# The order of maxima, scores and values on TensorE in two attention layers, and which wait an exponential carries

## What is computed

```python
scores = jnp.einsum('bhqd,bhkd->bhqk', q, k) / jnp.sqrt(jnp.float32(HEAD_DIM))
causal = jnp.tril(jnp.ones((t, t), dtype=bool))          # first layer only
scores = jnp.where(causal[None, None], scores, -jnp.inf)
attn = jax.nn.softmax(scores, axis=-1)
out = jnp.einsum('bhqk,bhkd->bhqd', attn, v)
```

## Time and profile before

| what | value |
|---|---|
| median of 3 runs | 5455.3 us (5450.6 to 5481.5) |
| the profiled execution's own time | 5454.2 us |
| its span | 5452.2 us |
| PE busy | 5027.6 us, 92% |
| DVE busy | 4536.7 us, 83% |
| ACT busy | 3758.9 us, 69% |
| reductions of maxima, line 915 | 3200, 3759.0 us, mean 1192 ns |
| exponentials, line 898 | 6400, 3384.1 us, mean 583 ns |

### The profile page before, as it was taken

One profiled execution on the slowest core, in us unless ns is written; L12 is line 12 of the kernel. 1 busy time (PEld: TensorE's weight loads), 2 busy tenths in 40 slices (PEclk: granted clock), 3 DMA queues, 4 the chain that ended last, 5 costly groups with the idle time before them and its releaser, 6 DMA issues. The chain is left out here.

```text
span 5452.2 us, 101966 instructions
## 1 busy us (share of the span) xinstructions
PE 5027.6 (92%) x42036; PEld 2060.9 (38%) x42036; DVE 4536.7 (83%) x5138; ACT 3758.9 (69%) x7157; POOL 308.2 (6%) x450
## 2 busy tenths in 40 slices
PE   7699999999999588878999999999999999999777
PEld 4333433433333255543333333333333333333433
DVE  3678889889875489759999999999999999997435
ACT  2177788777777322224888888888888888888523
POOL 3100000000000011130000000000000000000200
PEclk7599999999988699987999999999999999999988
DMA  4300010010000000060100001000100000000000
GB/s 128 104 28 21 14 36 14 11 42 8 10 7 10 21 14 12 22 207 10 42 7 4 5 18 28 7 5 7 34 12 7 2 7 7 4 8 2 4 9 27
DMA packets 138199, 131.28 MB, mean 24 GB/s; under 512 B 61802, under 2 KB 96490, under 8 KB 137706
## 3 DMA queue, kind: packets, MB, share of 16 engines
q1 hardware_dynamic: 137738, 124.80, 7.7%
HBM read 76.75 MB, written 46.66 MB: 23 GB/s over the span
## 5 line engine op out<-in xcount | busy, mean ns | idle before, releaser
L915 DVE TENSOR_REDUCE att_mx<-ps 128x2 f32<-128x1024 f32 (+2 forms) x3200 | 3759.0, 1192 | 310.5 <-PE ps L801 203.8
L898 ACT ACTIVATE att_probs<-ps 128x512 f32<-128x512 f32 (+3 forms) x6400 | 3384.1, 583 | 656.2 <-PE ps L839 562.9
L864 PE MATMUL ps<-att_probs,att_V 128*17 128x256 f32 (+1 forms) x25088 | 1970.2, 389 | 0.2
L839 PE MATMUL ps<-att_Q,K 50*128 50x512 f32 (+3 forms) x6400 | 1736.0, 497 | 50.7 <-ACT att_probs L898 29.6
L801 PE MATMUL ps<-K,att_Q 48*128 48x512 f32 (+2 forms) x6400 | 1434.7, 416 | 91.3 <-DVE att_mx L915 54.8
L839 PEld LDWEIGHTS ps<-att_Q,K 50*128 50x128 f32 x6400 | 685.0, 186 | 1416.3 <-ACT att_probs L898 1261.6
L864 PEld LDWEIGHTS ps<-att_probs,att_V 128*17 128x17 f32 x25088 | 427.3, 96 | 1077.4 <-issue 609.3
L801 PEld LDWEIGHTS ps<-K,att_Q 48*128 48x128 f32 x6400 | 677.8, 194 | 173.1 <-DVE att_mx L915 121.8
L726 POOL TENSOR_SCALAR_AFFINE_SELECT att_probs<-att_probs 128x512 f32<-128x512 f32 x128 | 81.2, 635 | 1554.8 <-ACT att_probs L898 1554.8
L1169 PE MATMUL ps<-wguT,mlp_xqT 128*128 128x512 f32 (+1 forms) x384 | 159.2, 565 | 0.6 <-DVE mlp_h L1277 0.2
L1351 POOL MEMSET mix_power<- 128x1 f32 x1 | 0.1, 98 | 2684.9 <-POOLq L131 2684.9
(11 more groups left out here) (209 smaller groups left out, 2436.8 us busy)
## 6 DMA issues: line engine op xcount, KB each, us to landing
att_Q<-qhi_scratch SPq DMA_DIRECT2D x256, 64.0 KB, 2.3
K<-khi_scratch SPq DMA_DIRECT2D x256, 64.0 KB, 2.3
v_scratch<-proj_vpad SPq DMA_DIRECT2D x16, 544.0 KB, 3.5
att_V<-v_scratch SPq DMA_DIRECT2D x64, 136.0 KB, 2.4
att_Q<-qlo_scratch SPq DMA_DIRECT2D x128, 64.0 KB, 2.3
K<-klo_scratch SPq DMA_DIRECT2D x128, 64.0 KB, 2.3
proj_x<-in_L_attn_x SPq DMA_DIRECT2D x8, 512.0 KB, 5.1
qhi_scratch<-proj_qhipart SPq DMA_DIRECT2D x16, 256.0 KB, 3.0
```

The source lines that it names most:

```text
L839: mm = pe.matmul(ring(at)[:, lo:QB], K[rows, par_of(u), j, kt * P:(kt + 1) * P], Q[rows, slot_of(u), j, lo:QB], start=True, stop=True)
L864: mm = pe.matmul(ps[VW * h:VW * h + HV, 6, lo:(part + 1) * (QB // 2)], V[:, par_of(v), kt, HV * h:HV * (h + 1)], probs[:, (n_key[v] + kt) ...
L898: act.activation(probs[:, (n_key[u] + kt) % PBUFS, column(h), lo:QB], ring(at)[:, lo:QB], ACT.Exp, scale=SCALE).then_inc(emptied, 1)
L915: dve.tensor_reduce(mx[:, min(u % NQB, 1), :, j, qt, c], ps[:, 2 + 2 * pair:4 + 2 * pair, 0:max_width(u, i) // 2], AX.X, ALU.max).then_inc ...
```

## The change

It has two parts. In `order(u)`, a maximum's slot is rounded down to an even one, and the maxima of a slot (and `gather` after the last of them) stand ahead of that slot's score instead of behind it. The list of a full stretch becomes: maximum, score, score, values. As the gather's slot is now even, `turn_max`, still five slots behind and still after its slot's score, comes after the second score of a pair, one group of steps earlier. On ScalarE, the wait on `scored` moves ahead of the waits on `values_done` and `out_read`, so it is the one that the exponential, or the copy of the output, carries.

```diff
-            at.append(min(int(slot) | 1, slots - 1))
+            at.append(min(int(slot) // 2 * 2, slots - 2))
...
             for h in range(GH):
-                out.append(("score", kt, h))
                 slot = kt * GH + h
                 for k, item in enumerate(todo):
                     if at[k] == slot:
                         out.append(("max", *item))
                         if k == last:
                             out.append(("gather",))
+                out.append(("score", kt, h))
                 if slot == gather_at + 5:
                     out.append(("turn_max",))
...
                         what = step[0]
+                        if what in RING:
+                            act.wait_ge(scored, at + 2)
                         if what == "score" and step[2] == 0:
 
                             act.wait_ge(values_done, n_key[u] + step[1] + 1)
                         if what == "turn_out":
                             act.wait_ge(out_read, step[1] + 1)
-                        if what in RING:
-                            act.wait_ge(scored, at + 2)
```

## The result

The changed kernel takes 5414.2 us (median of 8, 5389.4 to 5441.6) where the kernel before, run beside it, takes 5459.4 (median of 8): a ratio of 0.991, interval 0.988 to 0.994. 5417 was predicted. In the executions beside the experiments the kernel before has the same median, 5459.

A forecast was written before the change was run, and what follows sets the result against it. TensorE's own sequence was taken to set the pace. Terms summed to -24 us in the second attention and -13 in the first: 5454.2 - 37 = 5417 us, range 5375 to 5465 (the forecast's own 5390 to 5430).

The forecast's parts named there:

- Point 1: TensorE's group order, maximum ahead of scores: same matmuls and loads, 0 us, bounds 0.02 either way per group.
- Point 2: Load of a pair's second score, held until 0.20 into the next group, is covered before its matmul at 0.34: 0 us.
- Rival A: The held second-score load finds no cover, groups 1.27 instead of 1.23: 5560 us, half covered 5502; chance 0.09.
- Point 3: Exponentials carry the wait for their scores, saving TensorE 0.02 per key tile: -19 us second attention, -7 first.
- Point 4: turn_max after a pair's second score, no longer between the two, saves 0.20 per unit: -6 us second attention, -4 first.
- one group of 1.72: Sign named for a right forecast: in the second attention, a transpose group of 1.72 us.
- Point 5: After turn_out, second maximum waits 0.20 in the open: +6, +4 us; copy no longer delays an exponential: -3, -2.
- Units of 79.9: Sign named for a right forecast: second attention's units of about 79.9 us instead of 81.0.
- Point 6: Last unit, without maxima, loses 2 us; at the first attention's seams, shorter waits for small loads and exponentials: -4.
- Rival B: VectorE's interruptions cost more, the gather too leaving an open wait of 0.4 in 62 units: +25, 5442 us; chance 0.21.
- Rival C: Denser seams in the first attention avoid most falls of TensorE's clock: another -30, 5387 us; chance 0.12.
- Rival D: The change does nothing: 0.02 per tile is given back at another wait, turn_max costs as before; 5450 us, chance 0.08.

The follow-up runs named there:

- e2: Kernel before with only ScalarE's wait on the scores moved, order of steps as before; 5397.3 us, ratio 0.989.
- e4: Changed kernel with met waits put between the wait for the scores and the exponential, holding exponentials 0.05 us longer; 5453.5 us.
- e9: Changed kernel with the wait for the scores put ahead of one more instruction, so a pair's first exponential is held longer; 5584.2 us, ratio 1.020.
- e7: Changed kernel with turn_max put back between two scores of a pair, six slots behind the gather instead of five; 5418.4 us.
- e3: Changed kernel with VectorE's division put behind its next reduction; 5407.7 us, ratio 0.989.
- e1: Kernel before with the new order of steps alone, ScalarE's waits as they were; 5459.7 us, ratio 1.001.
- e6: Kernel of e5 with the next unit's maxima, gather and transpose four slots earlier in each unit; 5408.4 us.
- e5: Kernel before with ScalarE's new wait, old order, and turn_max four slots behind the gather instead of five; 5382.0 us, ratio 0.989.
- e12: The kernel of e5 measured again; 5379.7 us, ratio 0.985.

## Why the prediction was right, and where only its sum was

The forecast's time was met (5414 for 5417), and the second attention fell by 24.2 where 24 was worked out. But the experiments show that not each step was right, and that part of the agreement is luck. By part of the change, the sum had -33 us for the wait, 0 for the order and -4 at the seams; measured at equal clock are -44 for the wait alone and +8 for the order on top of it.

**Point 1, the order at 0 us.** Confirmed for plain groups: e2 with scores ahead and after with a maximum ahead both have 1.22 (1.221 in both without the groups of 1.4 and more). But the order is more than its plain groups. In each unit's third key tile, two pairs stand without values between them, and ScalarE also copies the output that was kept (line 908) there. The prediction has no term for this place. Timeline of after:

```profile
4007.40 0.50 PE L801 MATMUL ps<-K,att_Q 48*128 48x512 f32 x2
...
4008.67 0.59 ACT L908 ACTIVATE att_outT<-ps 128x512 f32<-128x512 f32 x1
4008.83 0.18 PEld L839 LDWEIGHTS ps<-att_Q,K 50*128 50x128 f32 x1 [0.52 <-ACT att_probs L898]
...
4010.40 0.50 PE L801 MATMUL ps<-K,att_Q 48*128 48x512 f32 x2
```

From the head at 4007.40 to the next at 4010.40 it is 2.99 (the rows' starts are rounded); it was 2.89 before and is 2.83 in e2. The order costs 0.16 here.

**Point 2, the held load is covered.** Right, to the hundredth: it begins 0.20 into the group and costs nothing, and the edge lies at 0.235 (e4, e9). Rival A had the right mechanism and price for what lies beyond it: the change passes the edge with 0.035 to spare. The rule that the prediction takes from the Trainium skill, page "TensorE: Matmul & The Clock Gate", Part 3, The mechanism, would hide nothing of this load. The trace disagrees: the loads at 4000.18 begin while the maximum's matmuls on the same rows run (4000.07, 0.50 long), and the scores still start at their place, 0.34. The same section of the Trainium skill also lets a load run ahead when it goes to the background weight buffer. The prediction left that out, and no run here speaks against it.

**Point 3, the exponential carries its wait.** Right in mechanism, and worth more than its term, since e2 shows that it is the whole gain. The exponentials' lag, 0.04 or 0.10, is 0.04 in all. In the second attention e2 takes 0.80 from the unit: 58 plain groups lose 0.0116 each, 0.67, and the groups at the third tile and after `turn_out` another 0.06 and 0.05. Forecast were 31 x 0.02 = 0.62.

**Point 4, turn_max.** 0.20 was forecast, 0.24 measured: the two groups take 3.13 in e2 and e7, whose exponentials carry the same wait, and 1.50 + 1.39 = 2.89 in the kernel after. Timeline of the kernel after, the transpose's group (first two rows) and the next:

```profile
3434.72 0.50 PE L801 MATMUL ps<-K,att_Q 48*128 48x512 f32 x2
...
3435.41 0.33 PE L811 MATMUL ps<-ident,att_negp 128*128 128x128 f32 x1
...
3436.23 0.19 PEld L801 LDWEIGHTS ps<-K,att_Q 48*128 48x128 f32 x2 [0.42 <-DVE att_mx L915]
3436.34 0.48 PEld L839 LDWEIGHTS ps<-att_Q,K 50*128 50x128 f32 x2
...
3436.57 0.56 PE L839 MATMUL ps<-att_Q,K 50*128 50x512 f32 x2
...
3437.62 0.50 PE L801 MATMUL ps<-K,att_Q 48*128 48x512 f32 x2
```

0.28 lies at the transpose (0.26 forecast) and 0.17 at the next pair's second score. 0.23 was forecast for that, with the load at 0.43 and covered up to 0.20; it comes at 3436.34 + 0.48 - 0.19 - 3436.23 = 0.40 and is covered up to 0.235. The place where I looked for it, one group of 1.72, was wrong: it is split over two.

**Point 5, turn_out.** The open wait is there at the size that was worked out. Timeline of after; the transposes, ScalarE's copy, the reductions behind the division, and the second maximum after it:

```profile
3532.84 0.66 PE L873 MATMUL ps<-ident,att_outT 128*128 128x128 f32 x4
3533.53 0.60 ACT L903 ACTIVATE att_out<-ps 128x512 f32<-128x512 f32 x1
...
3534.79 3.48 DVE L915 TENSOR_REDUCE att_mx<-ps 128x2 f32<-128x1024 f32 x3
...
3536.07 0.19 PEld L801 LDWEIGHTS ps<-K,att_Q 48*128 48x128 f32 x2 [0.62 <-DVE att_mx L915]
```

Its load is at 3536.07, 3.23 after the transposes, as forecast; the idle time before it is 0.62 where a plain group has 0.42, so 0.20 of open wait. The group before it is 1.42, in e2 1.25: 0.17. e3 took 0.15 of it from the unit, with 0.18 expected. The other half of this point, the copy that no longer delays an exponential, was put at 0.09 a unit; the group after `turn_out` fell from 1.30 to 1.25 in e2, of which 0.01 is the pace, so 0.04.

By unit, then, in the second attention, before to after: plain groups -0.67 (forecast -0.62), transpose -0.25 (-0.20; 3.15 before), open wait and copy together +0.12 (+0.20 - 0.09), third tile +0.10 (none). That gives -0.70; 80.71 to 80.00 is -0.71, and the forecast's own terms give -0.71 too. That is luck: a missing term of +0.10 was balanced by 0.05 more at the plain groups and 0.05 more at the transpose. (Units of 79.9 "instead of 81.0" in the prediction are a slip: 81.0 is the window of one unit, the median was 80.71.)

**Point 6, the last unit and the seams.** The last unit fell from 72.50 to 70.50, exactly the 2 of the forecast, and it did so in e2 too (70.5) and not in e1 (72.3): the wait alone. For the seams -4 was taken. The waits for the small loads in the first attention stand here first for the kernel before, then for after:

```profile
PEld ps L839 <- DMA att_Q<-att_negT: 15.9, 13, 2.2
PE ps L839 <- DMA att_Q<-att_negT: 13.4, 13, 4.3
```

```profile
PE ps L839 <- DMA att_Q<-att_negT: 8.5, 7, 4.4
PEld ps L839 <- DMA att_Q<-att_negT: 8.4, 9, 1.2
PEld ps L801 <- DMA att_Q<-att_negT: 5.4, 4, 1.4
PE ps L801 <- DMA att_Q<-att_negT: 3.4, 4, 0.9
```

29 before, 26 after: a part of it went from the scores to the maxima that now stand ahead. That 3 us less is within the -4, but no proof of it.

**The first attention** is where the sum was weakest. -13 was forecast. The profiled executions differ by 40, but 186.8 us were at half clock before and 102.0 after, and by the slope above a microsecond at half clock goes with 0.4 us of time (44 us for 0.01 of 5440, which is 109 us at half speed). Without that part it is, as an estimate, 1552.2 - 75 = 1477 before and 1511.9 - 41 = 1471 after: -6. e2 gives 1519.4 - 53 = 1466, -11, and e1 1546.3 - 64 = 1482, +5. So the wait brought some 11, near the 13 that were forecast for it with the copy and the seams, and the order took back half of it. The step that was mis-sized is the order's part in this attention: the sum had +4 for the maxima's wait and -4 for the earlier transpose, 0 in all. The view of waits shows where, first attention, e2 and then after:

```profile
PEld ps L801 <- DVE att_mx L915: 26.7, 51, 1.1
```

```profile
PEld ps L801 <- DVE att_mx L915: 146.5, 326, 1.3
```

**Rival B** is what this looks like, confined to the units that host more maxima than they have pairs: there VectorE has no slack, and a maximum at the head of a group waits in the open with the scores behind it. A unit of that kind takes 32.5 at full clock before, 32.2 in e2 and 34.0 in e1. (The total includes the idle time that any load has before it, as the 0.42 of a plain group; the units' times are the better measure.) In full units of the second attention B did not come: the maximum after the gather is in time, but for the place in e7. Its weight of 0.21 was for the gather everywhere; the error was to price it per unit and not per kind of unit.

**Rival C, the clock.** The execution that was profiled had 0.944 and 5389.4, what rival C gave (5387), but the eight executions of after reach from 0.931 to 0.944. e6 thinned the waits at the seams, and the clock was low for longer, not shorter. C is not confirmed.

**Rival D** is excluded by e2, whose units keep what the wait brings. (Its 5450 should be 5453 by the prediction's own terms.)

What the study does not settle: the cause of the clock's falls in the first attention, the execution's own share of the pace (1.214 or 1.223 for one kernel), and the long groups that come with a separate wait for the scores.

## What to carry to other kernels

Where an instruction has two waits, let it carry the one that is met last and leave the one that is met long before to the separate instruction ahead: the 0.06 us of the separate one then pass while the engine would wait in any case, and do not come on top of the last wait. On the engine that sets the pace, put a step whose release may come late behind work that can start without it: a maximum at the head of a group makes everything behind it wait for VectorE (0.20 after `turn_out`), and behind the scores the same wait is hidden. When a change has two parts, run each alone before the gain is put down to both: here one part gave 44 us at equal clock and the other took back some 8. And compare executions at the same granted clock when it moves the time as much as the change does.

## What the runs showed of the hardware that was not expected

- A held weight load is hidden up to an edge some 0.105 us ahead of its matmul's place. At 0.20 into the group it cost nothing (after), at 0.27 it cost 0.03 and at 0.30 it cost 0.065 in its group (e9).
- An exponential starts 0.04 us after its scores when it carries the wait for them (after), 0.086 to 0.10 when an instruction right ahead of it does (e4, before), and 0.16 when one more instruction stands between (e9).
- Two executions of one kernel, e5 and e12, had a pace of 1.214 and 1.223 through the whole second attention at full clock. 0.7% of pace is therefore no evidence for a kernel from one profile.
- 0.01 of the mean granted clock goes with 44 us over 135 executions, more than the 36 that the whole change is worth at equal clock.
